# A transformer layer on eight cores: the attention's exp over wide score tiles issued as two instructions, with its waits split by half

## The reference

```python
kqv = x @ Wqkv + bqkv
kqv = kqv.reshape(b, s, 3, NUM_HEADS, HEAD_SIZE)
q = kqv[:, :, 0]
k = kqv[:, :, 1]
v = kqv[:, :, 2]
scores = jnp.einsum('bsnh,btnh->bnst', k, q) / math.sqrt(HEAD_SIZE)
ones = jnp.ones_like(scores)
scores = jnp.triu(scores) + -10000.0 * jnp.tril(ones, k=-1)
attn = jax.nn.softmax(scores, axis=2)
out = jnp.einsum('bnkq,bknh->bqnh', attn, v)
out = out.reshape(b, s, NUM_HEADS * HEAD_SIZE)
return out @ Wo + bo
...
g = jnp.einsum('bsh,ih->bsi', hidden_state, Wg)
u = jnp.einsum('bsh,ih->bsi', hidden_state, Wu)
h = jax.nn.silu(g) * u
return jnp.einsum('bsi,hi->bsh', h, Wd)
```

## Time and profile before

| what | value |
|---|---|
| runs shown | 3054.53 and 3388.32 us, median 3221.42 us |
| the profiled execution | 3056.08 us |
| its span on the slowest core (core 7) | 3054.5 us |
| spans of the eight cores | 3040.9 to 3054.5 us |
| mean granted TensorE clock, by core | 0.932 to 0.937 |
| TensorE busy | 2454.5 us (80%) |
| VectorE busy | 946.7 us (31%) |
| ScalarE busy | 789.0 us (26%) |

### The profile page before, as it was taken

How to read it: one execution, slowest core, us unless ns; L and a number is a source line. 1 busy time by engine, 2 the same in 40 slices (tenths; PEclk the granted TensorE clock), 3 DMA queues, 4 the chain that set the end, 5 groups by cost and what they waited for, 6 DMA issues and landing times.

```text
span 3054.5 us, 31162 instructions; the slowest of 8 cores (3040.9 to 3054.5 us)
## 1 busy us (share of the span) xinstructions
PE 2454.5 (80%) x12624; PEld 1156.6 (38%) x12624; DVE 946.7 (31%) x1172; ACT 789.0 (26%) x1076; POOL 34.2 (1%) x61
## 2 busy tenths in 40 slices
PE   1256777777777787765555999999999999999998
PEld 0133333333434443332222444444444444444443
DVE  0354333333333333332233222222322222232222
ACT  0133333333333333331001312213030312213130
POOL 0000000000000000000000000000000000000000
PEclk9976999999999999977777999999999999999999
DMA  7744111111111211024442101101010101001012
GB/s 101 145 139 127 21 21 21 21 21 21 21 21 21 39 25 21 1 77 145 143 124 89 56 21 42 42 31 52 21 52 21 52 21 52 32 32 52 21 42 110
DMA packets 30860, 162.04 MB, mean 53 GB/s; under 512 B 2592, under 2 KB 2640, under 8 KB 23296
## 3 DMA queue, kind: packets, MB, share of 16 engines
q0 software_dynamic: 9600, 67.78, 10.1%
q1 hardware_dynamic: 20832, 90.71, 9.0%
q10 hardware_dynamic: 288, 1.57, 0.1%
HBM read 185.74 MB, written 16.78 MB: 66 GB/s over the span
## 4 chain that ended last, share of the span: by engine, by line
PE 70%; DVE 11%; ACT 7%; issue 6%; DMA 3%; another core or an unknown queue 2%; DVEq 0%; ACTq 0%; POOL 0%; POOLq 0%; SPq 0%
PE PB L183 36%; PE SC L183 14%; PE PJP L183 14%; DVE STAT L183 6%; PE TP L183 3%; PE OP L183 3%; DMA WOC<-wo_bf 2%; DVE YS L183 2%; ACT VF L183 1%; ACT PS L183 1%; ACT PT L183 1%; DVE SC L183 1%; DVE PS L183 1%; ACT PTB L183 1%
## 5 line engine op out<-in xcount | busy, mean ns | idle before, releaser
L183 PE MATMUL PJP<-XHF,WQKVB 128*128 128x512 bf16 x2048 | 488.5, 394 | 18.9 <-ACT KS L183 15.6
L183 PE MATMUL PB<-YF,GD 128*128 128x512 bf16 x2048 | 459.8, 383 | 21.0 <-DVE YS L183 18.3
L183 PE MATMUL PB<-YF,UD 128*128 128x512 bf16 x2048 | 452.5, 379 | 0.0
L183 PEld LDWEIGHTS PJP<-XHF,WQKVB 128*128 128x128 bf16 x2048 | 206.2, 101 | 276.9 <-issue 67.2
L183 PEld LDWEIGHTS PB<-YF,GD 128*128 128x128 bf16 x2048 | 201.6, 99 | 269.9 <-issue 34.4
L183 DVE SCALAR_TENSOR_TENSOR HBUF<-PB,USC,SIG 128x1024 bf16<-128x1024 f32 x64 | 82.2, 1284 | 684.9 <-PE PB L183 684.9
L183 PEld LDWEIGHTS PB<-YF,UD 128*128 128x128 bf16 x2048 | 200.3, 98 | 241.7
L183 ACT ACTIVATE SIG<-PB,GSC 128x1024 f32<-128x1024 f32 x64 | 71.3, 1114 | 741.0 <-PE PB L183 741.0
L183 PE MATMUL SC<-DDG,HBUF 128*128 128x512 bf16 x1024 | 226.2, 379 | 12.4 <-DVE HBUF L183 12.4
L183 PE MATMUL PB<-DDG,HBUF 128*128 128x512 bf16 x1024 | 226.2, 379 | 0.0
L183 PE MATMUL OP<-PS,VS 128*128 128x128 bf16 x1152 | 126.9, 236 | 106.9 <-DVE PS L183 52.2
(11 more groups left out here) (68 smaller groups left out, 1641.2 us busy)
## 6 DMA issues: line engine op xcount, KB each, us to landing
GUD<-u_blob SPq DMA_DIRECT2D x62, 768.0 KB, 4.3
WQKVB<-f_blob POOLq DMA_DIRECT2D x16, 1536.0 KB, 11.8
XT<-x_full SPq DMA_DIRECT2D x16, 1024.0 KB, 6.1
WOC<-wo_bf SPq DMA_DIRECT2D x16, 1024.0 KB, 5.5
WOC<-wo_bf POOLq DMA_DIRECT2D x16, 1024.0 KB, 6.3
wo_bf<-f_blob POOLq DMA_DIRECT2D x1, 8192.0 KB, 96.2
XT<-x_q SPq DMA_DIRECT2D x8, 1024.0 KB, 5.2
YS<-x_q POOLq DMA_DIRECT2D x8, 1024.0 KB, 5.1
```

Of the source, the lines that this page charges most:

```text
L183: r = getattr(e, meth)(*args, **kw)
```

## The change

For tiles j >= 4 the exp is issued as two ACTIVATEs, over columns 0 to 1023 and 1024 to `ext`, each with a row sum of its own; a VectorE `tensor_tensor` adds the two sums ahead of the reciprocal, and the reciprocal waits for it. The one wait of QK for all earlier exps becomes a wait ahead of each 512-column matmul, for the exp that last read that half. Tiles j <= 3 are as before.

```diff
--- before.py
+++ after.py
@@ -526,6 +526,7 @@
     tap("XQF", XQF[:, :], [128, NCH * 1024], BF16, [xqf_done])
 
     sc_rel = None
+    sc_hrel2 = [None, None]
     sc_half_rel = [None, None]
     os_rel = None
     ps_rel = [None, None]
@@ -609,12 +610,14 @@
                                   q_ready[h]])
             else:
                 off = 0
-                p.wait("tensor", [sc_half_rel[0], sc_half_rel[1], sc_rel,
-                                  ks_ready[h], q_ready[h]])
+                p.wait("tensor", [ks_ready[h], q_ready[h]])
             SCV = SC[:, off:off + ext]
             ev_qk = None
             for seg in range(0, ext, 512):
                 seg_w = min(512, ext - seg)
+                if j > 3:
+                    hf = seg // 1024
+                    p.wait("tensor", [sc_half_rel[hf], sc_hrel2[hf]])
                 ev_qk = p.op("tensor", "matmul", SCV[:, seg:seg + seg_w],
                              QH[par][:, j * 128:(j + 1) * 128],
                              KS[par][:, seg:seg + seg_w],
@@ -631,15 +634,29 @@
                          negate=True, inc=SV)
             pbuf = (h * QT + j) % 2
             p.wait("scalar", [ev_mx, pt_rel[pbuf]])
-            ev_exp = p.op("scalar", "activation", PT[pbuf][:, 0:ext],
-                          SCV[:, 0:ext],
-                          AF.Exp, bias=mneg, scale=1.0, accum_out=ssum,
-                          inc=SS)
             if j <= 3:
+                ev_exp = p.op("scalar", "activation", PT[pbuf][:, 0:ext],
+                              SCV[:, 0:ext],
+                              AF.Exp, bias=mneg, scale=1.0, accum_out=ssum,
+                              inc=SS)
                 sc_half_rel[j % 2] = ev_exp
+                p.wait("vector", ev_exp)
             else:
-                sc_rel = ev_exp
-            p.wait("vector", ev_exp)
+                ssum2 = STAT[:, sl + 3:sl + 4]
+                ev_e0 = p.op("scalar", "activation", PT[pbuf][:, 0:1024],
+                             SCV[:, 0:1024],
+                             AF.Exp, bias=mneg, scale=1.0, accum_out=ssum,
+                             inc=SS)
+                sc_hrel2[0] = ev_e0
+                ev_exp = p.op("scalar", "activation", PT[pbuf][:, 1024:ext],
+                              SCV[:, 1024:ext],
+                              AF.Exp, bias=mneg, scale=1.0, accum_out=ssum2,
+                              inc=SS)
+                sc_hrel2[1] = sc_rel = ev_exp
+                p.wait("vector", ev_exp)
+                ev_sa = p.op("vector", "tensor_tensor", ssum, ssum, ssum2,
+                             ALU.add, inc=SV)
+                p.wait("vector", ev_sa)
             ev_ri = p.op("vector", "reciprocal", rinv, ssum, inc=SV)
             p.wait("vector", ev_ri)
             ev_pn = p.op("vector", "tensor_scalar_mul", PT[pbuf][:, 0:ext],
@@ -685,6 +702,7 @@
     woc_rel = [[attn_last], [attn_last]]
     pj_rel = [[sc_rel, sc_half_rel[0], sc_half_rel[1]],
               [sc_rel, sc_half_rel[0], sc_half_rel[1]]]
+    assert sc_rel is sc_hrel2[1]
     ev_y = {}
     ytm_rel = [None, None]
     yf_done = None
```

## The result

| | before | changed kernel |
|---|---|---|
| median of the runs | 3056.92 us | 3083.97 us |
| profiled execution | 3056.08 us | 3080.20 us |
| span of the slowest core | 3054.5 us (core 7) | 3078.6 us (core 5) |
| granted TensorE clock, by core | 0.932 to 0.937 | 0.929 to 0.931 |

The ratio of the runs is 1.0077, with a 95% interval of 1.0066 to 1.0089: 20 to 27 us slower, where 18 us were forecast. That is within 2% and clear of zero.

What follows compares the result with a forecast made beforehand. TensorE, at 70%, was taken as the bound, with the exp on the path through ScalarE's queue. Tile terms 3.9 + 2.5 + 0.3 + 5.5 + 3.9 and head 15's 1.9 gave 18.0 us: 3056.1 to 3074 us, range 3048 to 3102.

Steps and rivals of the forecast that it cites:

- The split wait costs and gives nothing: QK on TensorE: its 256 matmuls have 0.0 us idle time before them, so the finer wait lets nothing start sooner.
- ScalarE's part: Second exp on ScalarE: 0.26 us a tile, bounds 0 and 2 x 0.26 us; some 17 us more busy time.
- VectorE's part: Add of the two row sums on VectorE: 0.27 us with its wait, bounds 0.16 and 0.54 us, partly covered by idle time.
- Head 15, 1.9 us: Last head, with no projections beside it: both parts count, 3 x 0.53 us, and 0.3 us in j=6.
- The idle time of the V transposes: TensorE's idle time ahead of the transposes of V: a sign, to grow from 74.2 us by 8 to 12.
- the loads of the next head's weights and of Wo are issued early and stay hidden: Weight loads around the attention: claimed to stay hidden, with no term in the sum.
- the split does what it says: Rival: QK starts two matmuls sooner in 64 tiles, at most 28 us against a cost of 18: 3046 us; 5%.
- A change of rhythm can move all 15 towards either end: TensorE's clock spells across 15 heads: bounds 17 us more or 27 us less, no change taken.
- the heads at 71.4 us: Sign for the forecast: from first exp to first exp a head takes 71.4 us in the mean.
- The clock rival: Rival: longer gaps make TensorE's clock fall once more in projection matmuls of j=4, 5, 6: 3138 us, +2.7%; 5%.

## Where the prediction was right, and the step that failed

- *The split wait costs and gives nothing.* Right. QK's idle time is 0.0 us before and after, and TensorE's instructions are the same.
- *ScalarE's part, 0.26 us a tile.* Right: 2.20 us in place of 1.95 from exp to QH. ScalarE's busy time rose by 805.3 - 789.0 = 16.3 us, against "some 17".
- *VectorE's part, 0.27 us with its wait.* Right: the add takes 159 ns, 0.26 us from start to start. That the tiles cover most of it held too: the add alone cost nothing that can be measured. (By the rule of the Trainium skill, page VectorE: DVE Perf Modes, section The DRAIN you can't avoid, measured there on copies, the wait would cost nothing extra. Here 0.26 us pass from start to start for an instruction of 0.16; no run takes the wait away, so what part of this is the wait's is not shown. By the prediction's own terms the sum would then be some 2.2 us smaller, not below 2.)
- *Head 15, 1.9 us.* Right, tile by tile: from exp to exp j=4 takes 8.22 us against 7.71, j=5 9.69 against 9.18, j=6 9.86 against 9.62, and j=7, to the end of its OS copy, 10.77 against 10.27. That is 1.76 us more on the slowest cores.
- *The idle time of the V transposes, 74.2 us and 8 to 12 more.* A little less came, 6.9 us.
- *"... the loads of the next head's weights and of Wo are issued early and stay hidden."* For Wo this is not so, in either kernel: TensorE waits for WOC<-wo_bf for 38.8 us in all before and 42.1 us in the changed kernel, each on its slowest core. They stand behind the attention and shift with it, so the sum is not touched beyond these 3.3 us between two executions.
- *The rival "the split does what it says", at most 28 us.* That counts two matmuls of 0.22 us; at its own 0.43 us it would be 55 us. With an idle time of 0.0 neither was there to be had.
- *"A change of rhythm can move all 15 towards either end ... These are bounds; I take no change."* This is the step that failed: the term for the clock was put at nothing, and with it the heads at 71.4 us. The heads were not 1.07 us longer but 1.42, on the cores' mean: 15 x 0.35 = 5 us, about the difference between 18.0 and the measured 23.5. The clock's spells were taken for a scatter that the mean head carries along unchanged. In its place the runs show two changes that the sum has not: the heads that were already at a clock of 0.93 grew by 0.65 us only, and the 46 of 112 that had 0.95 or 0.97 before all but disappeared, which makes 0.8 us a head. None of this was in the sum, so that 18 us came as near to 23.5 as it did is in part luck. The runs with known delays show that they answer to the delay: 0.28 us gives 0.2, 0.47 gives 1.0, and from 0.9 to 2.1 us the mean head only moves between 71.5 and 71.7. So the error has no fixed sign: with three exps the same sum is 18 + 16 = 34 us, and 22 were measured.
- *The clock rival, slower by over 2%.* It named the right resource and the wrong form. A spell more did come, but only in the heads that were short before, 46 of 112; none of heads 1 to 14 had a granted clock below the 0.93 of the long heads.

What stays open: why the step lies near 71.7 us. The windows show that in step the heads have their low clock at the same places, and heads in pairs, threes and fours, which nothing in the kernel's work asks for, speak for a timing of the clock's own; this was not tried, since nothing in the kernel sets it.

## What to carry to other kernels

Ask first whether a wait is waited on: an idle time of 0.0 before the waiting group, and a program in which the wait has been left out as already covered, make a finer wait worth nothing, and the instructions that it needs are then the whole effect. What made the exp costly was not its result's reader but its neighbour in the in-order queue; moving the neighbour (0.979) was worth more than anything done to the exp. And where TensorE's clock goes up and down in a loop, do not add small delays up. Take the granted clock of each turn of the loop: where some turns have a higher one than others, a small delay can cost the difference between them, and where all have the lowest already, as here at 71.7 us, a further delay can cost nothing.

## What was not expected of the hardware

- Turns of a loop with spells of low TensorE clock settle at one length: 71.67 to 71.71 us for heads 6 to 14 on all eight cores of the changed kernel with 0.18 us more, a mean of 71.69 us without it, and a mean of 71.68 us with 1.0 us more.
- The add alone, 64 instructions more, came with a shorter mean head, 70.03 against 70.27 us, in one execution of each; its ratio of 0.9993 takes in 1. Work of 0.1 us a head has no sign here that can be told.
- One-column ACTIVATEs overlap on ScalarE: five in a row take 0.56 us from the first's start to the last's end and hold up what follows by 0.46 us, some 0.09 us each. The expectations took them by the duration of a row, at 0.2 to 0.3 us each.
